# Second cross attention of a fused decoder block: scores from split keys and queries in three products, low parts on VectorE, and the last layer norm's steps in other places

## The chip, the cores and the metric

One core of a Trainium2 chip runs the whole program, one launch. The metric is the device time in microseconds (us). The times quoted are medians over runs of the same kernel. The engines are TensorE (PE, with its weight loads PEld), VectorE (DVE), ScalarE (ACT), GpSimd (POOL) and SyncE (SP, which issues DMAs here).

## What is computed

`x` is 8 batches of 256 rows of 256 features. Four residual blocks follow each other: a cross attention, a self attention with a mixture of experts, a second cross attention, and a feed-forward. The change is about the third, with its tail end in the layer norm ahead of the fourth and its preparation in the experts' stage:

```
q = rms_norm(x @ wq)                 # 16 heads of 128, rotary afterwards
k = rms_norm(x @ wk); v = x @ wv     # 4 key/value heads, 4 query heads share one
k_ctx = rms_norm(ctx @ wk_ctx)       # 64 context keys, no rotary
scores = q . concat(k_ctx, k) / sqrt(128) + causal mask on the last 256
out = softmax(scores) @ concat(v_ctx, v);  x = x + tanh(g) * (out @ wo)
x = x + tanh(g2) * ffn(layernorm(x))
```

Scores are wanted at close to full fp32 precision.

## The kernel before, in words

Stage "x1" is the second cross attention. It has 32 steps (`NI`), one for each pair of a key/value head `g = i // 8` and a batch `i % 8`; a step does the four query heads `h` of that pair. The order on every engine is written out by hand: each engine's function has a loop over `i`, and in it work for step `i` (softmax, values, output projection), `j = i + 1` (transposes of queries and keys, first scores) and `k = i + 2` (projections, rotary) is mixed. Engines meet by semaphores in the dictionary `q`; a wait blocks everything behind it on the same engine.

Products that must be precise are done with split operands: `three` adds high x high, high x low and low x high, where the high part is the operand rounded to float32r (lines L293 to L295). Where an operand isn't split, a plain fp32 matmul is issued. Before the change the scores (`scores`, L1798 and L1800) are two plain fp32 products for a head: 128 queries against 192 keys and 128 queries against 320 keys (64 context keys with 128 or 256 own ones). Stationary is the query block, moving are the keys.

The way of a query to its scores: `proj_q` on PE, `take_q` on DVE, `sum_q` on POOL, `q_tr` (four transposes for each half `t`) on PE into one of the two PSUM banks `pT`, `q_ev` (L1689) on ACT copies it to SBUF as `x_qT`. Keys go the same way by `rotate_k`, `sum_k`, `k_tr`, `k_ev` (L1696, `x_kT`); context keys are put into `x_kT` by POOL (`context_keys`, L1725). The softmax of a head is `scores` (PE), `soft` (DVE L1997), `exp` (ACT L1913), `recip` (DVE L2005), `normalise` (ACT L1921), `p_tr` (PE L1808), `p_ev` (ACT L1907), `p_low` (DVE L2010). Then `attend` (PE), `o_ev` (ACT), `o_low` (DVE L2016), `out_proj` (PE), `add_out` (DVE L2023). All transposes share the two `pT` banks in the order of the table `turns`; `bank_free` makes a transpose wait until the bank's former content has been read.

Steps 26 to 31 also carry the layer norm of the next stage, for one batch each: statistics (`norm.stats`, DVE), inverse (`norm.inverse`, POOL L190 and L192), rows (`norm_rows`, DVE L197), transposes (`norm_tr`, PE), a copy and a rounding (`norm_ev`, ACT L1941 and L1944), the low part (`norm_low`, POOL L2103).

The stage ahead, "moe", ends with the projections and transposes of step 0. At its start SP issues the loads of the experts' second bias (`moe_b`), the context and its key and value weights, tables, and of `moe_xs` (L2204).

Of the kernel before, what the change touches and what calls it, by code (L numbers as in the profile page):

```python
# [31 lines left out]
G = 4  # L32
# [38 lines left out]
def build(nc, d, out, spill, stop=99):  # L71
    ctx = ExitStack()
    with ctx:
# [1496 lines left out]
        Head = namedtuple("Head", "q QR qT kT Vh Vl KR nrq at_p at_qk bank_free place proj_kv proj_q q_tr k_tr take_kv squares q_ev k_ev "  # L1570
                          "take_q rotate_k context_keys inverse_norm_k sum_k sum_q inverse_norms_q t2")

        def cross_head(scope, KT, tables):
# [12 lines left out]
            qT = sb("x1_qT", [P, HG, S], F32, scope)  # L1586
            kT = sb("x1_kT", [P, 2, 2 * SC + S], F32, scope)
# [4 lines left out]
                     "vz", "vs", "vsf", "vsh", "pl")  # L1592
# [92 lines left out]
            def q_ev(e, i, t):  # L1685
# [3 lines left out]
                e.activation(qT[:, :, t * P:(t + 1) * P], pT[:, c % 2, :].rearrange("p (h n) -> p h n", h=HG),  # L1689
                             ACT.Copy).then_inc(q["te"], 1)  # L1690

            def k_ev(e, i):
# [3 lines left out]
                e.activation(kT[:, i % 2, SC:SC + S], pT[:, c % 2, 0:S], ACT.Copy).then_inc(q["te"], 1)  # L1696
# [57 lines left out]
            return Head(q, QR, qT, kT, Vh, Vl, KR, nrq, at_p, at_qk, bank_free, place, proj_kv, proj_q, q_tr, k_tr, take_kv, squares, q_ev,  # L1754
                        k_ev, take_q, rotate_k, context_keys, inverse_norm_k, sum_k, sum_q, inverse_norms_q, t2)

        def cross_attention_1(scope, head, KT, VC, mask, w_here, cw_here, w_next, cw_next):
# [3 lines left out]
            (q, QR, qT, kT, Vh, Vl, KR, nrq, at_p, at_qk, bank_free, place, proj_kv, proj_q, q_tr, k_tr, take_kv, squares, q_ev, k_ev, take_q,  # L1761
# [4 lines left out]
            WO = KD * (GW + 2 * HD)  # L1766
            VS = sb(name + "_VS", [P, T, HD], F32, scope)
# [11 lines left out]
            xa = KT[:, 2, :].rearrange("p (k n) -> p k n", k=KD)  # L1779
# [14 lines left out]
            def pe(e):  # L1794
                def scores(i, h):
                    e.wait_ge(q["te"], at_qk(i, 2) + 1)
                    e.wait_ge(q["sct"], pos(HG * i + h - 1))
                    e.matmul(pS[:, h % 2, 0:SC + P], qT[:, h, 0:P], kT[:, i % 2, SC + P:2 * SC + S],  # L1798
                             start=True, stop=True)
                    e.matmul(pS[:, h % 2, SC + P:2 * SC + P + S], qT[:, h, P:S], kT[:, i % 2, 0:SC + S],  # L1800
                             start=True, stop=True).then_inc(q["sc"], 1)
# [10 lines left out]
                def attend(i, hp):  # L1812

                    m = PR * i + hp
                    e.wait_ge(q["pl"], HG * i + 2 * hp + 2)
# [45 lines left out]
                for i in range(NI):  # L1861
# [28 lines left out]
                    if i >= 26:  # L1890
                        norm_tr(i - 26)
                    p_tr(i, 3)
                    if one:
                        scores(j, 1)
                    if two:
                        proj_q(e, k, 1)
# [5 lines left out]
            def act(e):  # L1902
# [34 lines left out]
                def norm_ev(b):  # L1937
                    c = place["norm", b]
                    e.wait_ge(q["tr"], c + 1)
                    e.wait_ge(q["nlo"], b)  # L1940
                    e.activation(xa, pT[:, c % 2, :].rearrange("p (k n) -> p k n", k=KD), ACT.Copy  # L1941
                                 ).then_inc(q["te"], 1)
                    e.wait_ge(q["te"], c + 1)
                    e.activation(XTh[:, :, columns(b)], xa, ACT.Copy).then_inc(q["nhi"], 1)  # L1944
# [5 lines left out]
                for i in range(NI):  # L1950
# [23 lines left out]
                    if i >= 26:  # L1974
                        norm_ev(i - 26)
# [5 lines left out]
                    if one:  # L1981
                        exp(j, 1)
                    o_ev(i, 1)
# [4 lines left out]
            def dve(e):  # L1988
# [18 lines left out]
                def p_low(i, h):  # L2007
# [3 lines left out]
                                    ).then_inc(q["pl"], 1)  # L2011
# [14 lines left out]
                def norm_rows(b):  # L2026
# [829 lines left out]
```

## Time and profile before

| | us |
|---|---|
| median of three runs (1768.93 to 1772.77) | 1770.06 |
| the profiled execution, as timed | 1772.32 |
| its span in the trace | 1770.5 |

| engine | busy us | share |
|---|---|---|
| PE | 1667.2 | 94% |
| PEld | 1514.9 | 86% |
| ACT | 1309.1 | 74% |
| DVE | 1181.1 | 67% |
| POOL | 1128.4 | 64% |

The shares are means over stages of different kinds. Stage x1 runs from 1083.19 us of the span to about 1652 us. For a stage made of equal steps the thing to read is one step: which engine has no idle time in it, and which waits of the others lead back to it. Matmuls are pipelined, so a PE record is longer than the time to the next start; what a matmul costs in a stream is start to start.

### The profile page before, as it was taken

What the parts mean: (1) busy time and instruction counts of PE and PEld (TensorE: products, weight loads), DVE (VectorE), ACT (ScalarE), POOL (GpSimd) and SP (SyncE); (2) the same over time, 40 slices, a digit from 0 to 9 for tenths busy, and PEclk for the clock granted to TensorE, in tenths of its full rate; (3) what the DMA queues carried; (4) which work ended last, traced back from release to release, by engine and by line L of the source; (5) the groups of instructions that cost most, each with busy time, mean ns of one, the idle gap of its engine ahead of it and who ended that gap; (6) DMA issues with size and microseconds to landing.
All of it is one profiled execution on the core that took longest, in us unless ns stands there. A gap on an engine that the chain in (4) does not pass through costs nothing.

```text
span 1770.5 us, 35509 instructions
## 1 busy us (share of the span) xinstructions
PE 1667.2 (94%) x11136; PEld 1514.9 (86%) x11136; DVE 1181.1 (67%) x3199; ACT 1309.1 (74%) x4211; POOL 1128.4 (64%) x1287
## 2 busy tenths in 40 slices
PE   6899998799999999999997997999999999988898
PEld 3788887688999999999986885999999999977897
DVE  5567678577776666566776786777777777776322
ACT  5677777598888888878874555889889898888221
POOL 5445546899999989898952215565565565665455
PEclk8999999899999999999998998999999999999999
DMA  4111211100000000000002010000000000000000
GB/s 147 50 42 34 70 28 59 38 19 13 19 19 13 24 15 19 14 19 13 13 7 95 20 30 8 13 13 9 13 9 12 13 9 19 19 17 8 10 19 25
DMA packets 32842, 45.88 MB, mean 26 GB/s; under 512 B 5264, under 2 KB 21904, under 8 KB 32656
## 3 DMA queue, kind: packets, MB, share of 16 engines
q1 hardware_dynamic: 32656, 43.59, 8.2%
q8 instruction: 93, 1.52, 0.4%
q14 instruction: 93, 0.76, 0.1%
HBM read 39.39 MB, written 4.19 MB: 25 GB/s over the span
## 4 chain that ended last, share of the span: by engine, by line
PE 73%; POOL 8%; DVE 8%; ACT 6%; issue 4%; DMA 1%; SPq 0%; POOLq 0%; DVEq 0%; ACTq 0%
PE pA L293 5%; PE pA L294 5%; PE pA L295 5%; PE pS L1112 4%; PE pF L293 4%; PE pF L295 4%; PE pF L294 4%; PE pS L1800 3%; PE pA L626 3%; PE pA L627 3%; PE pA L628 3%; PE pO L1131 3%; PE pF L827 3%; PE pT L1808 3%; PE pO L293 2%
## 5 line engine op out<-in xcount | busy, mean ns | idle before, releaser
L293 PE MATMUL pA<-Wh,XTh 128*128 128x512 f32 (+1 forms) x512 | 221.1, 432 | 7.8 <-SPq L119 4.2
L1533 POOL TENSOR_TENSOR f_sw<-f_sw,f_sin 128x512 f32<-128x512 f32 x128 | 181.9, 1421 | 34.1 <-ACT f_sw L1242 34.1
L294 PE MATMUL pA<-Wl,XTh 128*128 128x512 f32 (+1 forms) x512 | 188.9, 369 | 0.0
L295 PE MATMUL pA<-Wh,XTl 128*128 128x512 f32 (+1 forms) x512 | 188.6, 368 | 0.0
L1242 ACT ACTIVATE f_sw<-pA 64x512 f32<-64x512 f32 x256 | 151.8, 593 | 34.8 <-PE pA L628 31.0
L1536 POOL TENSOR_TENSOR f_sw<-f_sw,f_RB 128x512 f32<-128x512 f32 x128 | 169.5, 1325 | 10.0
L626 PE MATMUL pA<-XTh,Wh 128*128 128x256 f32 x512 | 163.8, 320 | 5.3 <-DVE f_qT L1385 5.3
L1913 ACT ACTIVATE x_P<-x_P,x_nm 128x192 f32<-128x192 f32 (+1 forms) x256 | 127.9, 505 | 51.7 <-DVE x_nm L1997 51.7
L1741 POOL TENSOR_TENSOR x_QR<-x_QR,x_t 128x512 f32<-128x512 f32 x64 | 82.1, 1283 | 118.6 <-DVE x_QR L1706 118.6
L628 PE MATMUL pA<-XTh,Wl 128*128 128x256 f32 x512 | 145.9, 285 | 0.0
L627 PE MATMUL pA<-XTl,Wh 128*128 128x256 f32 x512 | 145.8, 285 | 0.0
L1263 ACT ACTIVATE f_P<-f_P,f_nm 128x128 f32<-128x128 f32 (+1 forms) x256 | 114.0, 447 | 21.4 <-DVE f_nm L1402 21.3
L1921 ACT ACTIVATE x_P<-x_P,x_rs 128x192 f32<-128x192 f32 (+1 forms) x256 | 117.2, 515 | 10.5 <-DVE x_rs L2005 10.5
L293 PEld LDWEIGHTS pA<-Wh,XTh 128*128 128x128 f32 x512 | 98.0, 192 | 28.1 <-SPq L119 4.4
L1997 DVE CUSTOM_DVE_ANT_0 x_P<-pS,x_mask,x_nrq 128x192 f32<-128x192 f32 (+1 forms) x256 | 113.1, 478 | 7.1 <-PE pS L1800 4.2
L294 PEld LDWEIGHTS pA<-Wl,XTh 128*128 128x128 f32 x512 | 98.2, 192 | 19.0 <-issue 0.4
L2010 DVE TENSOR_TENSOR Wl<-pT,Wh 128x512 fp32r<-128x512 f32 x128 | 87.1, 680 | 38.1 <-ACT Wh L1907 37.9
L295 PEld LDWEIGHTS pA<-Wh,XTl 128*128 128x128 f32 x512 | 97.9, 191 | 17.1
L1402 DVE CUSTOM_DVE_ANT_0 f_P<-pS,f_mask 128x128 f32<-128x128 f32 (+1 forms) x256 | 80.7, 352 | 46.7 <-PE pS L1112 45.9
L1112 PE MATMUL pS<-f_kT,f_qT 128*128 128x128 f32 (+1 forms) x512 | 105.2, 328 | 3.9 <-POOL f_kT L1539 3.9
L626 PEld LDWEIGHTS pA<-XTh,Wh 128*128 128x128 f32 x512 | 98.7, 193 | 8.2 <-issue 5.7
L288 POOL TENSOR_TENSOR Wl<-RAW,Wh 128x384 fp32r<-128x384 f32 (+3 forms) x72 | 75.4, 1047 | 44.2 <-ACT Wh L281 27.4
(318 smaller groups left out, 6308.0 us busy)
## 6 DMA issues: line engine op xcount, KB each, us to landing
RAW<-in_w_f SPq DMA_DIRECT2D x32, 256.0 KB, 2.7
RAW<-in_w_x SPq DMA_DIRECT2D x32, 192.0 KB, 2.4
RAW<-in_w_x SPq DMA_DIRECT2D x32, 160.0 KB, 2.4
x_base<-in_w_x0b SPq DMA_DIRECT2D x20, 192.0 KB, 2.5
RAW<-in_w_ff SPq DMA_DIRECT2D x8, 288.0 KB, 2.8
R<-in_x SPq DMA_DIRECT2D x4, 512.0 KB, 6.8
x_spill<-R SPq DMA_DIRECT2D x8, 256.0 KB, 2.0
RAW<-in_w_moe SPq DMA_DIRECT2D x8, 256.0 KB, 2.7
```

The source lines that it names most:

```text
L293: e.matmul(o, ah, bh, start=first, stop=False)
L294: e.matmul(o, ah, bl, start=False, stop=False)
L295: return e.matmul(o, al, bh, start=False, stop=last)
L626: e.matmul(o[:, a * S:(a + 1) * S], Wh[g % 2][:, w], xh, start=(k == 0), stop=False)
L627: e.matmul(o[:, a * S:(a + 1) * S], Wh[g % 2][:, w], xl, start=False, stop=False)
L628: ins = e.matmul(o[:, a * S:(a + 1) * S], Wl[g % 2][:, w], xh, start=False, stop=(k == KD - 1))
L1112: ins = e.matmul(pS[:, h % 2, OFF[t]:OFF[t] + WID[t]], qT[:, i % 2, h, t * P:(t + 1) * P], kT[:, i % 2, h, 0:WID[t]], start=True, stop=True)
L1242: ins = e.activation(sw[dst, n, :, :], pA[src, n % 2, :].rearrange("p (a n) -> p a n", a=2), ACT.Copy)
L1533: e.tensor_tensor(y, y, bc(sind[:, :], 1, 2), ALU.mult).then_inc(q["swm"], 1)
L1536: e.tensor_tensor(y, y, RB[:, g % 2, 2 * n:2 * n + 2, :], ALU.add).then_inc(q["swb"], 1)
L1913: ins = e.activation(x, x, ACT.Exp, scale=-1.0, bias=nm[:, h, t:t + 1], accum_out=sm[:, h, t:t + 1])
L1921: ins = e.activation(x, x, ACT.Copy, scale=rs[:, h, t:t + 1])
```

## The change

Scores are computed by `three` from split operands. The ACT copies `q_ev` and `k_ev` now write the high parts `x_qTh` and `x_kTh` in float32r, and three new DVE instructions in a step write the low parts from PSUM: `q_low` twice (128x512) and `k_low` once (128x256). `scores` waits for them by the new semaphore `low`, which takes the place of `pl` and counts the low parts of all transposes in order of `turns`; `bank_free` waits for it too. POOL writes two instructions for the context keys in place of one. In the loop of DVE both `q_low` stand ahead of `rotate_k`, and `k_low` behind `p_low(i, 2)`. In the last six steps the norm's rows go from DVE to POOL, its low part from POOL to DVE (straight from PSUM, without the copy on ACT), and its transposes stand later in `turns`, on PE and on ACT. To make room in SBUF, the experts' second bias is loaded in four pieces, some of the experts' small tiles share memory, and the value weights of the context are loaded later, into the tile of the key weights.

```diff
@@ cross_head
-                turns += [("q", x, 2) for x in j] + [("norm", i - 26)] * (i >= 26) + [("p", i, 3)]
+                turns += [("q", x, 2) for x in j] + [("p", i, 3)] + [("norm", i - 26)] * (i >= 26)
+            def low_done(c):
+
+                return sum(x[0] != "norm" for x in turns[:c + 1])
             def bank_free(e, c):
 
                 e.wait_ge(q["te"], pos(c - 1))
-                if c >= 2 and turns[c - 2][0] == "p":
-                    e.wait_ge(q["pl"], HG * turns[c - 2][1] + turns[c - 2][2] + 1)
+                e.wait_ge(q["low"], low_done(c - 2) if c >= 2 else 0)
+                if c >= 2 and turns[c - 2][0] == "norm":
+                    e.wait_ge(q["nlo"], turns[c - 2][1] + 1)
...
+            def q_low(e, i, t):
+                c, x = at_qk(i, t), slice(t * P, (t + 1) * P)
+                e.wait_ge(q["te"], c + 1)
+                e.tensor_tensor(lows["q"][:, :, x], pT[:, c % 2, :].rearrange("p (h n) -> p h n", h=HG),
+                                qTh[:, :, x].bitcast(F32), ALU.subtract).then_inc(q["low"], 1)
+
+            def k_low(e, i):
+                c = at_qk(i, 2)
+                e.wait_ge(q["te"], c + 1)
+                e.tensor_tensor(kTl[:, i % 2, SC:SC + S], pT[:, c % 2, 0:S], kTh[:, i % 2, SC:SC + S].bitcast(F32),
+                                ALU.subtract).then_inc(q["low"], 1)
...
-                e.tensor_copy(kT[:, i % 2, :].rearrange("p (a n) -> p a n", n=SC)[:, ::5, :],
-                              bc(KT[:, g, b * SC:(b + 1) * SC], 1, 2))
+                e.tensor_copy(hi, own).then_inc(q["ckh"], 1)
+                e.wait_ge(q["ckh"], i + 1)
+                e.tensor_tensor(lo, own, hi.bitcast(F32), ALU.subtract)
@@ cross_attention_1, pe
                 def scores(i, h):
-                    e.wait_ge(q["te"], at_qk(i, 2) + 1)
+                    e.wait_ge(q["low"], low_done(at_qk(i, 2)))
                     e.wait_ge(q["sct"], pos(HG * i + h - 1))
-                    e.matmul(pS[:, h % 2, 0:SC + P], qT[:, h, 0:P], kT[:, i % 2, SC + P:2 * SC + S],
-                             start=True, stop=True)
-                    e.matmul(pS[:, h % 2, SC + P:2 * SC + P + S], qT[:, h, P:S], kT[:, i % 2, 0:SC + S],
-                             start=True, stop=True).then_inc(q["sc"], 1)
+                    for t, own in enumerate((slice(SC + P, 2 * SC + S), slice(0, SC + S))):
+                        r = slice(t * P, (t + 1) * P)
+                        ins = three(e, pS[:, h % 2, OFF[t]:OFF[t] + WID[t]], qTh[:, h, r], qTl[:, h, r],
+                                    kTh[:, i % 2, own], kTl[:, i % 2, own], True, True)
+                    ins.then_inc(q["sc"], 1)
@@ cross_attention_1, dve
                     soft(i, 3)
+                    if one:
+                        q_low(e, j, 0)
+                        q_low(e, j, 1)
                     if two:
                         rotate_k(e, k)
                     recip(i, 3)
-                    if i >= 26:
-                        norm_rows(i - 26)
                     o_low(i, 0)
                     p_low(i, 2)
+                    if one:
+                        k_low(e, j)
...
                     o_low(i, 1)
+                    if i >= 26:
+                        norm_low(i - 26)
@@ cross_attention_1, pool
                         sum_k(e, k)
+                    if i >= 26:
+                        norm.inverse(e, i - 26)
+                        norm_rows(i - 26)
                     w_low(i)
...
-                    if i >= 26:
-                        norm_low(i - 26)
-                    if 25 <= i < NI - 1:
-                        norm.inverse(e, i - 25)
@@ experts, sp
-                e.dma_start(b2[:, :], d["be2"].partition_broadcast(P)).then_inc(q["bias"], 16)
+                for x in range(E):
+                    e.dma_start(biases[x], d["be2"][x * D:(x + 1) * D].partition_broadcast(P)).then_inc(q["bias"], 16)
...
-                e.dma_start(wv, d["x1_Wv"].rearrange("(k p) n -> p k n", p=P)).then_inc(q["ctx"], 16)
...
+                    if i == 2:
+                        e.wait_ge(q["ck"], 4)
+                        e.dma_start(wv[:, :, :], d["x1_Wv"].rearrange("(k p) n -> p k n", p=P)).then_inc(q["wv"], 16)
@@ experts, dve, at its end
                 norm_rows(B - 1)
+                head.q_low(e, 0, 0)
+                head.q_low(e, 0, 1)
                 head.rotate_k(e, 1)
                 norm_low(B - 1)
+                head.k_low(e, 0)
```

What stands in a row on VectorE in the middle of an ordinary step, from the end of the fourth head's `soft` to `add_out`, before (L1715 to L1719 are `rotate_k`, L2005 is `recip`, L2016 `o_low`, L2010 `p_low`, L2023 `add_out`):

```order
L1997 ISA x_nm 128x1
L1715 SCALAR_TENSOR_TENSOR x_KR<-pA,x_ssk,x_cosk 128x128
L1717 SCALAR_TENSOR_TENSOR x_tk<-pA,x_ssk,x_sink 128x128
L1715 SCALAR_TENSOR_TENSOR x_KR<-pA,x_ssk,x_cosk 128x128
L1717 SCALAR_TENSOR_TENSOR x_tk<-pA,x_ssk,x_sink 128x128
L1719 TENSOR_TENSOR x_Vl<-pA,x_Vh 128x256
L2005 RECIPROCAL x_rs<-x_sm 128x2
L2016 TENSOR_TENSOR x_OTl<-pO,x_OTh 128x512
L2010 TENSOR_TENSOR Wl<-pT,Wh 128x512
L2023 SCALAR_TENSOR_TENSOR R<-pF,tanhg,R 128x512
```

The same place on VectorE in the changed kernel (its line numbers are some 15 to 25 higher; L1708 is `q_low`, L1714 is `k_low`):

```order
L2017 ISA x_nm 128x1
L1708 TENSOR_TENSOR x_qTl<-pT,x_qTh 128x4x128 x2
L1734 SCALAR_TENSOR_TENSOR x_KR<-pA,x_ssk,x_cosk 128x128
L1736 SCALAR_TENSOR_TENSOR x_tk<-pA,x_ssk,x_sink 128x128
L1734 SCALAR_TENSOR_TENSOR x_KR<-pA,x_ssk,x_cosk 128x128
L1736 SCALAR_TENSOR_TENSOR x_tk<-pA,x_ssk,x_sink 128x128
L1738 TENSOR_TENSOR x_Vl<-pA,x_Vh 128x256
L2025 RECIPROCAL x_rs<-x_sm 128x2
L2036 TENSOR_TENSOR x_OTl<-pO,x_OTh 128x512
L2030 TENSOR_TENSOR Wl<-pT,Wh 128x512
L1714 TENSOR_TENSOR x_kTl<-pT,x_kTh 128x256
L2043 SCALAR_TENSOR_TENSOR R<-pF,tanhg,R 128x512
```

Two 128x512 instructions came in ahead of the keys' rotation, and one of 128x256 behind the third head's low part; nothing else moved there.

On TensorE, at the first head's scores of the next step, between `out_proj` (pF) and `proj_q` (pA), before:

```order
L295 MATMUL pF<-Wh,x_OTl 128x256
L1798 MATMUL pS<-x_kT,x_qT 128x192
L1800 MATMUL pS<-x_kT,x_qT 128x320
L293 MATMUL pA<-Wh,XTh 128x512
L294 MATMUL pA<-Wl,XTh 128x512
```

The same place on TensorE in the changed kernel:

```order
L295 MATMUL pF<-Wh,x_OTl 128x256
L293 MATMUL pS<-x_kTh,x_qTh 128x192
L294 MATMUL pS<-x_kTl,x_qTh 128x192
L295 MATMUL pS<-x_kTh,x_qTl 128x192
L293 MATMUL pS<-x_kTh,x_qTh 128x320
L294 MATMUL pS<-x_kTl,x_qTh 128x320
L295 MATMUL pS<-x_kTh,x_qTl 128x320
L293 MATMUL pA<-Wh,XTh 128x512
```

Six products stand where two stood, and they now need the DVE rows L1708 and L1714 of the fence above; the neighbours are the same.

On GpSimd in one of the last six steps, from the queries' sums on, before (L2103 is `norm_low`, L190 and L192 `norm.inverse`, L1730 and L1732 the inverse norms of the keys for which `rotate_k` waits):

```order
L1741 TENSOR_TENSOR x_QR<-x_QR,x_t 128x512 x2
L1747 TENSOR_SCALAR x_nrq<-x_ssq 128x8
L1750 TENSOR_TENSOR x_nrq<-x_nrq,mhalf 128x8
L1752 TENSOR_SCALAR x_nrq<-x_nrq 128x8
L2103 TENSOR_TENSOR XTl<-x_KT,XTh 128x2x256
L190 TENSOR_SCALAR rstd<-mv 128x2
L192 TENSOR_TENSOR rstd<-rstd,mhalf 128x2
L1730 TENSOR_SCALAR x_ssk<-x_ssk 128x2
L1732 TENSOR_TENSOR x_ssk<-x_ssk,mhalf 128x2
```

And in the changed kernel, from the queries' inverse norms to the norm's work of the next step:

```order
L1774 TENSOR_SCALAR x_nrq<-x_nrq 128x8
L1752 TENSOR_SCALAR x_ssk<-x_ssk 128x2
L1754 TENSOR_TENSOR x_ssk<-x_ssk,mhalf 128x2
L2112 TENSOR_SCALAR x_VS<-x_VC,x_half 128x128 x2
L2116 CAST Wh<-x_VS 128x256
L2118 TENSOR_TENSOR Wl<-x_VS,Wh 128x256
L1746 CAST x_kTh<-x_KT 128x2x64
L1748 TENSOR_TENSOR x_kTl<-x_KT,x_kTh 128x2x64
L1758 TENSOR_TENSOR x_KR<-x_KR,x_tk 128x256
L190 TENSOR_SCALAR rstd<-mv 128x2
L192 TENSOR_TENSOR rstd<-rstd,mhalf 128x2
L197 TENSOR_SCALAR x_KT<-R,mv,rstd 128x256 x2
```

The low part and the inverse are gone from the place ahead of the keys' inverse norms; the inverse now stands with the rows behind the keys' sum.

## Rows read from the trace of the kernel before

**Rows 1.** Busy time (count) by engine in one step: start:end, length, PE to POOL, clock, DMA, GB/s.

```profile
1308.36:1325.26 16.90, 16.90 (x116) 15.38 (x115) 12.48 (x37) 15.10 (x56) 9.80 (x15) 1.00 0.04 11
```

**Rows 2.** Chain that ended last, 1300 to 1340 us: start, us, what.

```profile
1308.53 0.33 PE pS L1798 x2
1308.85 0.54 PE pS L1800 x2
...
1325.42 0.33 PE pS L1798 x2
```

**Rows 3.** Waits, 1110 to 1540 us: us in total, times, longest us.

```profile
ACT x_P L1913 <- DVE x_nm L1997: 32.8, 25, 1.3
```

**Rows 4.** Timeline of PE in a step: start us, us, engine, line, operation.

```profile
1308.36 0.49 PE L1798 MATMUL pS<-x_kT,x_qT 128*128 128x192 f32 x2
...
1309.46 0.39 PE L294 MATMUL pA<-Wl,XTh 128*128 128x512 f32 x1
...
1310.39 0.39 PE L295 MATMUL pA<-Wh,XTl 128*128 128x512 f32 x1
...
1317.08 0.28 PE L293 MATMUL pA<-Wh,XTh 128*128 128x256 f32 x1
...
1317.67 0.28 PE L295 MATMUL pA<-Wh,XTl 128*128 128x256 f32 x1
1317.80 0.60 PE L1808 MATMUL pT<-ident,x_P 128*128 128x128 f32 x4
```

**Rows 5.** Timeline of ACT, same step and the one before.

```profile
1301.52 0.60 ACT L1907 ACTIVATE Wh<-pT 128x512 fp32r<-128x512 f32 x1 [0.17 <-PE pT L1808]
...
1304.56 1.09 ACT L1689 ACTIVATE x_qT<-pT 128x512 f32<-128x512 f32 x2
...
1307.45 0.42 ACT L1696 ACTIVATE x_kT<-pT 128x256 f32<-128x256 f32 x1
...
1310.36 0.46 ACT L1913 ACTIVATE x_P<-x_P,x_nm 128x192 f32<-128x192 f32 x1 [1.34 <-DVE x_nm L1997]
...
1318.43 0.60 ACT L1907 ACTIVATE Wh<-pT 128x512 fp32r<-128x512 f32 x1 [0.16 <-PE pT L1808]
```

**Rows 6.** Timeline of DVE in the same step.

```profile
1305.00 0.35 DVE L1715 SCALAR_TENSOR_TENSOR x_KR<-pA,x_ssk,x_cosk 128x128 f32<-128x128 f32 x1 [0.86 <-POOL x_ssk L1732]
...
1306.05 0.42 DVE L1719 TENSOR_TENSOR x_Vl<-pA,x_Vh 128x256 fp32r<-128x256 f32 x1
...
1307.14 0.69 DVE L2016 TENSOR_TENSOR x_OTl<-pO,x_OTh 128x512 fp32r<-128x512 f32 x1 [0.32 <-ACT x_OTh L1928]
1307.75 0.68 DVE L2010 TENSOR_TENSOR Wl<-pT,Wh 128x512 fp32r<-128x512 f32 x1
...
1312.02 0.15 DVE L2005 RECIPROCAL x_rs<-x_sm 128x2 f32<-128x2 f32 x1
1312.10 0.67 DVE L2010 TENSOR_TENSOR Wl<-pT,Wh 128x512 fp32r<-128x512 f32 x1
1312.68 0.41 DVE L1997 CUSTOM_DVE_ANT_0 x_P<-pS,x_mask,x_nrq 128x192 f32<-128x192 f32 x1
```

**Rows 7.** Timeline where PE waited for ACT, first step of the stage.

```profile
1090.03 0.90 ACT L1921 ACTIVATE x_P<-x_P,x_rs 128x192 f32<-128x192 f32 x2
...
1090.98 0.33 PE L1808 MATMUL pT<-ident,x_P 128*128 128x128 f32 x1 [1.17 <-ACT x_P L1921]
```

**Rows 8.** Chain that ended last, 1540 to 1600 us, in the last six steps.

```profile
1556.85 1.68 POOL x_nrq L1750
1558.86 1.25 POOL XTl L2103
...
1576.60 1.68 POOL x_nrq L1750
```

**Rows 9.** Timelines of SP's issues and of DVE at the start of stage moe.

```profile
944.84 0.45 SPq L2204 DMA_DIRECT2D moe_xs<-x_spill  x1
...
951.93 1.79 DVE L2411 SCALAR_TENSOR_TENSOR moe_xs<-moe_b,moe_gcomb,moe_xs 128x256 f32<-128x256 f32 x2 [3.19 <-DMA moe_xs<-x_spill]
```

More of the change, by code:

```diff
@@ L1568, in feed_up @@
             ins.then_inc(ff_up["gu"], 1)
-        Head = namedtuple("Head", "q QR qT kT Vh Vl KR nrq at_p at_qk bank_free place proj_kv proj_q q_tr k_tr take_kv squares q_ev k_ev "
+        Head = namedtuple("Head", "q QR qTh kTh kTl lows low_done q_low k_low Vh Vl KR nrq at_p at_qk bank_free place proj_kv proj_q q_tr k_tr take_kv squares q_ev k_ev "
                           "take_q rotate_k context_keys inverse_norm_k sum_k sum_q inverse_norms_q t2")
@@ L1752, in inverse_norms_q @@
                 e.tensor_scalar(a, a, -1.0, None, ALU.mult).then_inc(q["rq"], 1)
-            return Head(q, QR, qT, kT, Vh, Vl, KR, nrq, at_p, at_qk, bank_free, place, proj_kv, proj_q, q_tr, k_tr, take_kv, squares, q_ev,
+            return Head(q, QR, qTh, kTh, kTl, lows, low_done, q_low, k_low, Vh, Vl, KR, nrq, at_p, at_qk, bank_free, place, proj_kv, proj_q, q_tr, k_tr, take_kv, squares, q_ev,
                         k_ev, take_q, rotate_k, context_keys, inverse_norm_k, sum_k, sum_q, inverse_norms_q, t2)
@@ L1760, in cross_attention_1 @@
             name = "x1"
-            (q, QR, qT, kT, Vh, Vl, KR, nrq, at_p, at_qk, bank_free, place, proj_kv, proj_q, q_tr, k_tr, take_kv, squares, q_ev, k_ev, take_q,
+            (q, QR, qTh, kTh, kTl, lows, low_done, q_low, k_low, Vh, Vl, KR, nrq, at_p, at_qk, bank_free, place, proj_kv, proj_q, q_tr, k_tr, take_kv, squares, q_ev, k_ev, take_q,
              rotate_k, context_keys, inverse_norm_k, sum_k, sum_q, inverse_norms_q, t2) = head
@@ L2024, in add_out, with norm_low @@
                                            ALU.mult, ALU.add).then_inc(q["acc"], 1)
-                def norm_rows(b):
-                    if b >= 2:
-                        e.wait_ge(q["tr"], place["norm", b - 2] + 1)
-                    else:
-                        e.wait_ge(q["rope"], NT * 8 * (G - 1))
-                    norm.rows(e, b)
+                def norm_low(b):
+                    c = place["norm", b]
+                    e.wait_ge(q["te"], c + 1)
+                    e.tensor_tensor(XTl[:, :, columns(b)], pT[:, c % 2, :].rearrange("p (k n) -> p k n", k=KD),
+                                    XTh[:, :, columns(b)].bitcast(F32), ALU.subtract).then_inc(q["nlo"], 1)
                 soft(0, 0)
@@ L2099, in w_low, with norm_rows @@
                     low_w(e, q["hi"], q["split"], cw_next if g == G - 1 else cw_here, i, i % 2, g % 2)
-                def norm_low(b):
-                    e.wait_ge(q["nhi"], b + 1)
-                    e.tensor_tensor(XTl[:, :, columns(b)], xa, XTh[:, :, columns(b)].bitcast(F32),
-                                    ALU.subtract).then_inc(q["nlo"], 1)
+                def norm_rows(b):
+                    if b >= 2:
+                        e.wait_ge(q["tr"], place["norm", b - 2] + 1)
+                    else:
+                        e.wait_ge(q["rope"], NT * 8 * (G - 1))
+                    norm.rows(e, b)
                 sum_q(e, 1, 0)
@@ L2402, in bias @@
                     if c == 0:
-                        e.wait_ge(q["bias"], 16)
+                        e.wait_ge(q["bias"], 64)
                         e.wait_ge(q["comb"], 1)
```

55 lines of the change are left out of this document (29 added, 26 removed).

## The prediction, made before the changed kernel ran

> **What bounds the kernel now.** I read the busy time by engine over one step first. In a step of the second cross attention PE has no idle time at all: 16.90 us of 16.90, at full granted clock, with ACT at 15.10, DVE at 12.48 and POOL at 9.80 [rows 1]. The reader is to see two things there: PE sets the step, and ACT has only 1.8 us of slack. The chain that ended last agrees: it repeats every 16.89 us, and the scores stand in it [rows 2]. Then the waits: the longest regular one of ACT is for `soft` of the next step's first head, 1.3 us at most, 25 times [rows 3]. So ACT's chain hangs on the moment at which PE gives those scores. The timelines of PE, ACT and DVE in one step then give the start of each instruction, which is all that the sum below needs [rows 4 to 6]. There are 32 steps: the first two, 25 equal ones (2 to 26), and the rest, which carry the norm in full.
>
> **The change, part by part.**
>
> *Scores, cost on PE.* Before, a head's scores take 0.33 + 0.54 = 0.87 us [rows 2]. After, they are three products of 192 columns and three of 320. What a split product costs start to start is seen at two sizes: 256 columns take 0.118 us (1317.08 to 1317.67 in five starts) and 512 take 0.2325 us (1309.46 to 1310.39 in four) [rows 4]. A line through both gives 0.147 us at 320 and 0.090 at 192. Nothing under 256 columns is in this trace in float32r, so 192 is unknown: at the low end 0.090 from the line, at the high end of what I call undisturbed 0.118 (it costs what 256 does), and, far off, the rate of plain fp32, 0.33 us for 192 columns [rows 2]. I take 0.109, near the upper of the close ends, because a weight load goes with each product. Then a head costs 3 x (0.109 + 0.147) = 0.77 us, 0.10 less than before; four heads make 0.40 us a step.
>
> The Trainium skill, page "TensorE: Matmul & The Clock Gate", section "LDWEIGHTS (loading the stationary operand)", gives columns / 1.2 ns for a load, which is 107 ns for the 128 columns here, more than the line's 90 ns. By the line the step below would come out 0.16 us shorter than by the load. The rows at 256 and 512 columns cannot tell the two apart.
>
> *Low parts, cost on DVE.* Two `q_low` have the shape of `p_low`, which takes 0.58 us start to start (1312.10 to 1312.68), and `k_low` has that of L1719, 0.42 us to its end [rows 6]. DVE has the room in total: 12.48 + 1.6 of 16.9. The cost is where they stand. They are on the way to the scores, and DVE is in order.
>
> *The new wait.* Take the step before as it ran. `k_ev` ended at 1307.45 + 0.42 = 1307.87 [rows 5], and PE began the scores at 1308.36, after its own work, without a wait [rows 4]. In the changed kernel the scores wait for `k_low`, which stands behind both `q_low`, all of `rotate_k`, `recip`, `o_low` and `p_low`. The first `q_low` waits for `q_ev`. So a cycle closes over one step, and I add it up, from first scores to first scores:
>
> 1. PE from the scores to the end of `p_tr` of the second head: 1308.36 to 1317.80 + 0.60 = 1318.40, that is 10.04 us [rows 4]. Three heads' scores lie in it, each 0.10 shorter: 9.74.
> 2. Hand-over to ACT 0.03 (`p_ev` starts at 1318.43). ACT from that `p_ev` to the start of the first `q_ev`: 1301.52 to 1304.56 = 3.04, and 0.61 for the copy itself (the row merges two, 1.09), then 0.03 to DVE: 3.71 in all [rows 5]. ACT is busy all through it.
> 3. DVE: two `q_low` 1.16; `rotate_k` 1305.00 to 1306.05 and the start to start of L1719, 0.34 (0.42 less the 0.08 overlap that DVE rows show): 1.39; `recip` 0.08 (1312.02 to 1312.10); `o_low` 0.61 (1307.14 to 1307.75); `p_low` 0.58; `k_low` 0.42. Together 4.24 [rows 6].
> 4. Hand-over to PE 0.05, from the place where PE waited for ACT (1090.03 + 0.90 to 1090.98) [rows 7].
>
> The sum is 9.74 + 3.71 + 4.24 + 0.05 = 17.74 us. The small waits on the way (the keys' transposes now need the second `q_low`) add some hundredths: I take 17.8. PE's own work would be 16.5, so PE stands idle 1.3 us in each step ahead of the first scores. Behind that wait on PE stand the projections of step k, `p_tr` of the fourth head and the second scores; ACT, which already waits 1.3 us for the first head [rows 3], waits some 2 us. The step grows by 0.9, and 25 of them by 22.5 us. The bounds: 0.090 for 192 columns gives 17.65 (nine products on the path), 0.118 gives 17.9. That is 25 x 0.75 to 25 x 1.0, or 19 to 25 us. The first two steps have the wait once or so: +0.5.
>
> *The last steps.* The chain there runs over POOL and repeats in 1576.60 - 1556.85 = 19.75 us, with the norm's low part (1.25) in it [rows 8]. That low part and the inverse leave POOL's path ahead of the keys' inverse norms, and ACT loses a copy. In exchange the new cycle of 17.8 us holds here too, with the norm's low part and statistics, 0.6 and 1.0 us, on DVE ahead of the next `p_low`. Between 17.8 and 19.4; I take 19.3, a gain of about 0.4 in some three or four steps, since the stage's tail has other limits: -1.2 us. Bounds: -7 and 0.
>
> *Loads and other small parts.* The first `moe_xs` is issued at 944.84, and DVE waits 3.19 us for it [rows 9]. Four bias loads in place of one add three issues of 0.45 us ahead, the removed value weights take one away: issued 0.9 later, with 0.5 MB less in front. I take 0, bounds -1 and +1. The value weights now come between the weight stream's third and fourth issue on SP; what they could hold back is needed a batch later. At the end of that stage two `q_low` fit into DVE's wait for the keys' inverse norms, and `k_low` adds 0.4 us: +0.2. POOL's extra instruction for the context keys, under 0.5 us, lies in its 7 us of idle time; with that cover gone it would cost 0.5 a step.
>
> **The sum.** 22.5 + 0.5 - 1.2 + 0.2 = 22; as the rounding of 17.74 to 17.8 may give 1.5 us too much, I forecast +21. The profiled execution took 1772.32 around a span of 1770.5, and so would become 1793.3; the median of the runs is 1770.06, 2.3 below it, and becomes 1791. With the bounds of the parts: 1783 to 1798.
>
> **Rivals.**
>
> *The scores' narrow products run at plain fp32's rate.* Then a product of 192 columns costs 0.33 us, a head 3 x (0.33 + 0.147) = 1.43, 0.56 more than before. Three heads on the path make the cycle 17.74 + 3 x 0.66 = 19.7, +2.85 a step, 71 us over 25; with the first and last steps some 82 us: 1852. For it: every product of `three` in the trace has 256 or 512 columns, so nothing excludes it. Against: nothing in the two sizes that are there hints at a step, since half the columns take half the time. A milder form, 0.16 us (two cycles for a column, one plain fp32 record), gives 17.74 + 0.48 = 18.2: +34 us with the ends, 1804.
>
> *The wait for the low parts is hidden, and PE stays the bound.* Then each step loses 0.40 us and 32 steps 13 us: 1757, faster. It needs the cycle to be under 16.5 us, 1.3 less than I count. It decides from the point at which DVE gives `k_low` before PE has done `out_proj`, 1308.36 in the step shown; by the sum DVE gives it 1.3 us later. For it: PE is the full engine and DVE has 4 us idle. Against: that idle time lies in other places, and DVE's starts are fixed by ACT's copies. The Trainium skill, page "FP8 and Floating Point Precision", section "TensorE Precision Notes", has true fp32 as four passes; with three products in place of four passes it speaks for a gain of a quarter of the scores' time. The trace agrees with four (192 columns in 0.33 us are 4.1 cycles a column), but the quarter is spent on PE, which would wait.
>
> *The cycle is as long, but half of the growth is hidden*, as `rotate_k` no longer waits for POOL and other waits close up: within 0.2% of 1770.
>
> **Chances.** The cycle as summed 0.74; the milder form of narrow products 0.06; plain fp32's rate 0.13; hidden wait, faster, 0.04; within 0.2% 0.03. A measurement of this kernel can tell about 0.2% (3.5 us) from no change. All but the last two are slower: 0.93. The range 1783 to 1808 takes in the likeliest case with its own range (1783 to 1798) and the milder form, 0.8 together; the far form is left out.
>
> **What the changed profile would show.** Right: steps of 17.8 us at equal distance; PE idle some 1.3 us once a step, ended by DVE's low part of the keys; DVE's `rotate_k` starting without a wait for POOL; scores of a head in 0.77 us; DVE at 14 of 17.8. The narrow products are read directly, start to start. Wrong: PE full in the steps (the wait is hidden), or an idle time that another instruction ends, or last steps that grow. What would make the sum wrong is above all an ACT that catches up while PE waits, since part 2 of the cycle is 3 us of its work, and a 192-column product outside 0.09 to 0.12.

## The result, and the profile after

The changed kernel takes 1789.68 us (median of 4 runs, 1786.65 to 1790.73), the kernel before 1770.24 (4 runs): the ratio is 1.0105, 95% interval 1.0088 to 1.0123. The forecast was 1791.0. The profiled execution of the changed kernel took 1788.75 us around a span of 1786.9. Of the kernels below, one profiled execution, that of norm_only, was disturbed (granted clock 0.65) and is not read.

One step between two of its equal neighbours, busy time by engine (start:end, length, PE to POOL, clock, DMA, GB/s), the counterpart of [rows 1]:

```profile
1317.26:1335.13 17.87, 16.82 (x123) 15.80 (x123) 13.72 (x40) 15.16 (x55) 10.24 (x16) 1.00 0.03 10
```

A step has grown from 16.90 to 17.87 us at the same clock, and PE is no longer full. The waits in the equal steps, 1120 to 1540 us (us in total, times, longest), say on what it stands:

```profile
ACT x_P L1936 <- DVE x_nm L2017: 54.5, 24, 2.3
...
PEld pS L293 <- DVE x_kTl L1714: 30.1, 24, 1.3
PE pS L293 <- DVE x_kTl L1714: 25.1, 24, 1.1
```

Once a step PE waits for the keys' low part. ACT's wait for the first head's softmax has grown from 1.3 [rows 3] to 2.3. The chain that ended last (start, us, what) shows one turn of the cycle:

```profile
1299.39 0.36 PE pS L293
...
1308.82 0.45 PE pT L1831 x4
1309.32 0.46 issue
1309.78 1.08 ACT x_P L1936 x4
...
1311.65 0.79 ACT x_P L1944 x2
1312.44 0.50 ACT x_qTh L1696
1312.96 0.52 DVE x_qTl L1708
...
1314.17 0.34 DVE x_KR L1734
...
1316.31 0.47 issue
1316.79 0.43 DVE x_kTl L1714
1317.26 0.36 PE pS L293
```

Read from the top: scores, PE's work to the second head's transposition, ACT's in-order work to the copy of the queries, then on VectorE the two `q_low`, the rotation, `o_low` and `p_low` (in the issue pieces), `k_low`, and the scores again, 17.87 us later. Without the wait the pieces from 1312.96 on could run beside PE; high_only, below, shows how far they do.

### The profile page after: what moved, and what is told of

Its sections match the earlier page's. It is cut to its first block, busy times and chain, and to the rows that moved or that the text cites. A ratio compares the mean times of both kernels' runs of the same rounds, so it can differ in the third digit from the quotient of the medians.

```text
span 1786.9 us, 36146 instructions
## 1 busy us (share of the span) xinstructions
PE 1660.5 (93%) x11392; PEld 1526.4 (85%) x11392; DVE 1220.4 (68%) x3289; ACT 1306.2 (73%) x4205; POOL 1149.5 (64%) x1325
## 4 chain that ended last, share of the span: by engine, by line
PE 64%; DVE 12%; ACT 10%; POOL 7%; issue 7%; DMA 0%; SPq 0%; POOLq 0%; DVEq 0%; ACTq 0%
PE pA L293 5%; PE pA L294 5%; PE pA L295 5%; PE pS L1112 4%; PE pA L626 3%; PE pA L628 3%; PE pA L627 3%; PE pO L1131 3%; PE pF L827 3%; PE pS L293 3%; PE pF L293 2%; PE pF L295 2%; PE pF L294 2%; ACT x_P L1936 2%; PE pT L1831 2%
## 5 line engine op out<-in xcount | busy, mean ns | idle before, releaser
L293 PE MATMUL pA<-Wh,XTh 128*128 128x512 f32 (+1 forms) x512 | 198.5, 388 | 8.1 <-SPq L119 4.2
L294 PE MATMUL pA<-Wl,XTh 128*128 128x512 f32 (+1 forms) x512 | 188.3, 368 | 0.0
L295 PE MATMUL pA<-Wh,XTl 128*128 128x512 f32 (+1 forms) x512 | 187.9, 367 | 0.0
L293 PE MATMUL pS<-x_kTh,x_qTh 128*128 128x192 f32 (+1 forms) x256 | 86.8, 339 | 35.6 <-DVE x_kTl L1714 32.1
L293 PEld LDWEIGHTS pA<-Wh,XTh 128*128 128x128 f32 x512 | 97.7, 191 | 21.1 <-SPq L119 4.4
L295 PEld LDWEIGHTS pA<-Wh,XTl 128*128 128x128 f32 x512 | 97.3, 190 | 17.0
L294 PEld LDWEIGHTS pA<-Wl,XTh 128*128 128x128 f32 x512 | 97.8, 191 | 11.3
```

The lines of the kernel that those rows point to most:

```text
L293: e.matmul(o, ah, bh, start=first, stop=False)
L294: e.matmul(o, ah, bl, start=False, stop=False)
L295: return e.matmul(o, al, bh, start=False, stop=last)
```

## Experiments

The twelve runs follow in the order in which they were made; "step" is the distance of one keys' transposition from the next in the 25 equal steps. The time of before beside them was 1771.2 us (the first four), 1771.9 (the next four) and 1770.9 (the last four); ratios are to it.

**high_only.** The scores' products read only high parts (the low parts' share of the scores is left out) and wait only for ScalarE's copies:

```diff
-                    e.wait_ge(q["low"], low_done(at_qk(i, 2)))
+                    e.wait_ge(q["te"], at_qk(i, 2) + 1)
-   three(e, ..., qTh[:, h, r], qTl[:, h, r], kTh[...], kTl[...], True, True)
+   three(e, ..., qTh[:, h, r], qTh[:, h, r], kTh[...], kTh[...], True, True)
```

> The changed kernel, but all three products of the scores read the high parts (the low parts' share of the scores is left out) and the scores wait only for the copies on ScalarE, no longer for the subtractions on VectorE; six matmuls a head and all subtractions stay. Theory (a step is the chain copy, subtraction, scores: TensorE's wait for the keys' low part, 1.3 us a step, is the cost): the wait goes, and a step falls from 17.87 to between TensorE's own busy time, 17.87 - 1.3 = 16.6, and the 16.90 of before; with some 30 steps the time is 1789.7 - 30 x 1.0 = 1760, between 1751 and 1765. Rival A (the three products themselves cost TensorE more than the two plain ones, because each needs a weight load of its own): the step stays near 17.9 and the time near 1790. Rival B (VectorE's three added subtractions, 1.6 us a step, delay its softmax work whether or not the scores wait for them): the step stays above 17.4, the time above 1775.

Measured: 1763.5 us, ratio 0.996 (0.9945 to 0.9976), step 16.92. The wait accounts for 0.95 of the 0.97 us; rival A falls. But PE is still not the bound. Its chain in a step still runs over VectorE:

```profile
1307.99 0.27 DVE x_kTl L1714
1308.32 0.74 DVE R L2043
1309.06 0.32 DVE x_P L2017
...
1310.26 0.73 ACT x_P L1936 x3
...
1311.51 0.70 DVE Wl L2030
1312.26 0.50 PE pO L293
```

The subtraction that nobody waits for still stands ahead of the sum into the rows and of the softmax of the next head. Rival B is right in kind, but small.

**f32_wait.** The products are plain fp32 again, of the high parts (the low parts' share is left out); the wait stays:

```diff
-   three(e, ..., qTh[:, h, r], qTl[:, h, r], kTh[...], kTl[...], True, True)
+   e.matmul(..., qTh[:, h, r].bitcast(F32), kTh[...].bitcast(F32), start=True, stop=True)
```

> The changed kernel, but the scores are two plain fp32 matmuls of the high parts again (the low parts' share is left out), while they still wait for both subtractions. Theory (the wait is the cost, and the three products are slightly cheaper than the plain ones): a head's scores go from 0.78 back to the 0.87 of before, the wait of 1.3 us stays, and a step takes 17.9 to 18.2, the time 1790 to 1800. Rival A (the products are the cost): the step is back at 16.9 and the time at 1770.

Measured: 1797.95 us, ratio 1.0154 (1.0138 to 1.0170), step 18.14. The wait alone costs 18.14 - 16.90 = 1.24 a step; the three products give back 0.27 of it, 0.09 for each of the three heads on the cycle.

**no_q_low.** Both `q_low` are left out, and the third product reads the high queries in their place (the diff shows the loop of VectorE alone):

```diff
-                    if one:
-                        q_low(e, j, 0)
-                        q_low(e, j, 1)
```

> The changed kernel without the two subtractions of the queries' low parts (the product of low queries with high keys reads the high queries in their place, so this share of the scores is left out); the keys' subtraction and its wait stay. Theory (all that stands on VectorE between ScalarE's copies and the keys' subtraction is on the cycle): two subtractions of 0.585 us start to start leave the cycle, 17.87 - 1.17 = 16.70, near TensorE's busy 16.6, and the time is 1789.7 - 30 x 1.17 = 1755, between 1748 and 1762. Rival (the keys' subtraction waits for its own copy on ScalarE, and the queries' lie in VectorE's idle time): the step stays above 17.6, the time above 1782.

Measured: 1772.9 us, ratio 1.001 (1.0001 to 1.002), step 17.20: 0.67 of the 1.17. The step falls only as far as the next way to the scores allows. Its chain reaches `k_low` over ScalarE's next exponential and copy:

```profile
1309.53 0.62 ACT x_qTh L1696
1310.14 0.75 ACT x_P L1935 x3
1311.11 0.50 ACT x_OTh L1950
1311.63 0.69 DVE x_OTl L2035
1312.43 0.41 issue
1312.84 0.43 DVE x_kTl L1714
1313.31 0.36 PE pS L293
```

**narrow.** Each product of 320 columns becomes one of 192 and one of 128:

```diff
-   for t, own in enumerate((slice(SC + P, 2 * SC + S), slice(0, SC + S))):
+   for t, a, n, at in ((0, SC + P, SC + P, OFF[0]), (1, 0, SC + P, OFF[1]), (1, SC + P, P, OFF[1] + SC + P)):
```

> The changed kernel with each product of 320 key columns split into one of 192 and one of 128: nine matmuls a head for six, the same columns in all, three more weight loads. In the trace of the changed kernel 192 columns take 0.110 us from start to start and 320 take 0.148. Theory W (below some width the weight load of about 0.107 us sets the distance, not the columns): 128 columns take 0.107 too, a head goes from 0.78 to 9 x 0.11 = 0.98, the four heads add 0.8 us of TensorE time a step; as 1.3 us of it was idle and one head's products lie on the cycle, a step takes 18.1 to 18.8, the time 1797 to 1817. Theory C (columns alone count, 0.110 x 128/192 = 0.073): a head goes to 0.88, at most 0.1 us more on the cycle, the time 1790 to 1794.

Measured: 1809.7 us, ratio 1.0222 (1.0204 to 1.0240), step 18.57. PE's timeline of one head (start, us, line, shape):

```profile
1310.04 0.27 PE L295 MATMUL pS<-x_kTh,x_qTl 128*128 128x192 f32 x1
1310.15 0.25 PE L293 MATMUL pS<-x_kTh,x_qTh 128*128 128x128 f32 x1
1310.23 0.27 PE L294 MATMUL pS<-x_kTl,x_qTh 128*128 128x128 f32 x1
1310.34 0.28 PE L295 MATMUL pS<-x_kTh,x_qTl 128*128 128x128 f32 x1
```

Over 200 us of this trace a product of 128 columns takes a median 0.112 us from start to start where L294 or L295 issues it (0.083 for L293's), one of 192 0.111: a third fewer columns bring nothing in two of three. A head has three more products and the step 0.70 us more, as theory W had it (theory C forecast at most 0.1). Theory W holds in kind. That the weight load is what holds them was not separated from another fixed cost.

**norm_only.** The kernel before with the norm's move alone:

```diff
-                    if i >= 26:
-                        norm_tr(i - 26)
                     p_tr(i, 3)
                     if one:
                         scores(j, 1)
+                    if i >= 26:
+                        norm_tr(i - 26)
...
-                    e.activation(xa, pT[...], ACT.Copy).then_inc(q["te"], 1)
-                    e.wait_ge(q["te"], c + 1)
-                    e.activation(XTh[:, :, columns(b)], xa, ACT.Copy).then_inc(q["nhi"], 1)
+                    e.activation(XTh[:, :, columns(b)], pT[...], ACT.Copy).then_inc(q["te"], 1)
```

(with `norm_rows` and `norm.inverse` on GpSimd and `norm_low` on VectorE, as in the change).

> The kernel before with only the norm's operations of its last six steps moved as in the change (its rows on GpSimd, one copy in place of two, its low part on VectorE out of the bank, its transposition behind the last head's scores); the scores stay plain. In the changed kernel the six steps and the tail took 4.6 us less than before beyond what the longer cycle does, where 1.2 was forecast. Theory (the move shortens the chain over GpSimd by itself): the time is 1770.2 - 4.6 = 1765.6, between 1763 and 1768. Rival (the gain came only because the changed kernel's steps are longer and hide the norm): 1769 to 1772, no difference.

Measured: 1762.1 us, ratio 0.9940 (0.9926 to 0.9955): 9.8 us faster, twice what was expected. Its steps are read in norm_only_b, below.

**rotate_last.** The keys' rotation behind the keys' subtraction:

```diff
-                    if two:
-                        rotate_k(e, k)
                     recip(i, 3)
                     o_low(i, 0)
                     p_low(i, 2)
                     if one:
                         k_low(e, j)
+                    if two:
+                        rotate_k(e, k)
```

> The changed kernel with the keys' rotation on VectorE (1.41 us, five instructions) behind the keys' subtraction, where it stood ahead of it; nothing is left out. Theory (what stands on VectorE between the queries' and the keys' subtraction is on the cycle, but the rotation is itself waited for by GpSimd's sum and then by the keys' transposition, which comes next): a step falls by a part of 1.41, to between 17.4 and 17.7, the time 1778 to 1787. Rival A (the whole 1.41 leaves the cycle, and TensorE's own 16.6 is the bound): 1752. Rival B (the rotation stood in idle time of VectorE): 1790, unchanged.

Measured: 1793.2 us, ratio 1.0125 (1.0110 to 1.0140): no gain on the changed kernel, whose interval ends at 1.0123. The step is 17.61, as the theory had it, 0.26 less than in the changed kernel and far from the 1.41 that was moved. What it left out are the last steps, at 20.87, 20.86, 20.85 and 21.99 us (19.04, 19.02, 19.03 and 18.56 in the changed kernel, so 8.9 more in all): the norm's rows on GpSimd wait behind the sum that needs the rotation.

```profile
1583.22 0.34 DVE x_Vl L1738
1583.63 0.74 POOL x_KR L1758
...
1584.73 0.73 POOL rstd L192
1585.64 2.44 POOL x_KT L197 x2
1588.22 0.63 PE pT L205 x4
```

**low_first.** Only work that nobody awaits at once is moved behind the subtraction:

```diff
-                    recip(i, 3)
-                    o_low(i, 0)
                     p_low(i, 2)
                     if one:
                         k_low(e, j)
+                    recip(i, 3)
+                    o_low(i, 0)
```

> The changed kernel with the last head's low part and the keys' subtraction moved on VectorE ahead of the reciprocal and the output's low part (0.08 + 0.60 us); the rotation stays ahead; nothing is left out. Theory (the same as of the rotation, with nothing that the moved operations are awaited for at once): a step falls by 0.68 to 17.2, the time 1789.7 - 30 x 0.68 = 1769, between 1766 and 1774, level with the kernel before. Rival (the keys' subtraction waits for its copy on ScalarE, which comes no earlier): 1785 to 1790.

Measured: 1772.7 us, ratio 1.0007 (0.9998 to 1.0017), step 17.21. Two moved instructions give back 17 of the 19 us.

**best_order.** ScalarE and VectorE in another order (one step, first and last calls left out):

```diff
                     squares(e, j, 1)
-                    p_ev(i, 1)
-                    exp(i, 2)
                     take_kv(e, k)
+                    p_ev(i, 1)
+                    exp(i, 2)
-                    normalise(i, 2)
                     q_ev(e, j, 0)
                     q_ev(e, j, 1)
-                    exp(i, 3)
+                    normalise(i, 2)
                     o_ev(i, 0)
                     p_ev(i, 2)
                     k_ev(e, j)
+                    exp(i, 3)
...
                     rotate_k(e, k)
-                    recip(i, 3)
-                    o_low(i, 0)
                     p_low(i, 2)
                     k_low(e, j)
-                    add_out(i - 1)
+                    recip(i, 3)
+                    o_low(i, 0)
```

> The changed kernel with another order of work on ScalarE and VectorE, nothing left out: ScalarE takes the projected keys before the second head's copy and copies the queries before the third head's normalisation, and the fourth head's exponential comes behind the copies of the keys; on VectorE the keys' subtraction comes before the reciprocal, the output's low part and the sum into the rows. Theory (the cycle of copy, subtraction, scores is what the three products cost, and shortening what stands in it gives it back down to TensorE's busy time and the 16.9 of before): a step takes 16.9, with the norm's 4 to 5 us the time is 1770.2 - 4.6 = 1765, or less, down to 1758, since the scores are cheaper at both ends too. Rival (another chain, that of ScalarE's 15.2 us busy with softmax and copies, closes at once behind it): 1770 to 1785.

Measured: 1764.5 us, ratio 0.9954 (0.9940 to 0.9968), step 16.95. `k_low` is still once a step on the chain. The kernel is faster than the one before, but not by its products: its step is no shorter than the 16.90 of before, and norm_only, with plain fp32 products, took 1762.1 beside it. What it gains on the kernel before is no more than the norm's move gives by itself.

**norm_only_b.** The same kernel as norm_only.

> The kernel before with only the norm's move, a second time, for the steps in its trace. The first time it took 1762.1, 9.8 less than before, where 4.6 was expected. Theory (before, the last steps were paced by GpSimd's chain of the norm at up to 19.7 us; without it they fall to TensorE's 16.9, while in the changed kernel they can fall only to that kernel's own 17.9 or more): the four steps that took 18.48, 19.72, 19.74 and 19.20 before take 17 to 18 each, the time is 1762 again. Rival (the gain lies behind the last step, or in another stage): these steps stay above 18.5.

Measured: 1759.6 us, ratio 0.9943 (0.9929 to 0.9956), so again 11 us faster. The four last steps take 17.73, 18.28, 18.27 and 18.00 us, 72.3 in all for 77.1 before. Some 4.6 us more are behind the last step: from its keys' transposition to the end it is 145.5 us for 150.1. One part of them is two waits of PE for the last low parts, 2.73 and 2.12 us before (the second shown, from PE's timeline) and 1.58 and 0.98 now, since a copy and a rounding of the norm stood ahead of ScalarE's last `p_ev`:

```profile
1643.16 0.54 PE L293 MATMUL pO<-Wh,x_Vh 128*128 128x512 f32 x1 [2.12 <-DVE Wl L2010]
```

```profile
1633.08 0.50 PE L293 MATMUL pO<-Wh,x_Vh 128*128 128x512 f32 x1 [0.98 <-DVE Wl L2008]
```

The other part is PE's granted clock. The windows of 11 us that begin 20 us behind the last keys' transposition, first of before and then of norm_only_b, have 0.84 and 1.00:

```profile
1640.45:1651.45 11.00, 7.05 (x42) 6.07 (x40) 2.27 (x4) 3.79 (x6) 1.67 (x2) 0.84 0.00 0
```

```profile
1632.53:1643.53 11.00, 6.97 (x51) 6.46 (x52) 3.42 (x6) 3.29 (x7) 1.74 (x4) 1.00 0.04 13
```

So have the next 11 us (1651.45 to 1662.45 before, 0.84; 1643.53 to 1654.53 now, 1.00). Counted from the last keys' transposition, PE is 2.2 us earlier behind the two waits, 3.6 behind the first window's stretch at the lower clock (512 columns at 0.43 us there) and 5.0 behind the second's (256 columns at 0.21 and not 0.12).

**products_only.** The changed kernel with the norm as before (the edit of norm_only, undone).

> The changed kernel with the norm's operations of the last six steps put back as they were before (rows on VectorE, two copies on ScalarE, low part on GpSimd, its transposition ahead of the last head's); the three products stay. Theory (its last steps were faster by less than those of the norm's move alone, since the three products' longer cycle runs through them): the time is 1789.7 + 4.6 = 1794.3, between 1792 and 1798, so the move is worth less here than the 9.8 that it brings alone. Rival (it is worth the same in both): 1789.7 + 9.8 = 1799.5.

Measured: 1803.6 us, ratio 1.0189 (1.0175 to 1.0203). Both expectations fall: the move is worth 13.9 us here (1803.6 - 1789.7; 13.3 to 14.9 by how the two runs of before are set off). The last four steps take 20.97, 22.11, 20.64 and 20.19 us. Two of them by windows:

```profile
1586.79:1608.90 22.11, 19.16 (x127) 17.48 (x127) 15.87 (x45) 16.59 (x59) 12.94 (x19) 0.92 0.05 14
1608.90:1629.54 20.64, 17.76 (x128) 16.16 (x127) 15.87 (x45) 16.49 (x59) 12.94 (x19) 1.00 0.06 15
```

and the chain through the first of them:

```profile
1581.96 1.68 POOL x_nrq L1770
1583.97 1.26 POOL XTl L2130
1585.58 0.73 POOL rstd L192
1586.68 0.71 POOL x_ssk L1752
...
1588.94 1.06 DVE x_KT L197 x2
...
1591.19 0.34 DVE x_kTl L1712
1591.58 0.53 PE pS L293
...
1593.39 0.43 PE pA L293
```

The two cycles join: GpSimd's norm work delays the keys' inverse norms, so the rotation, and `k_low` behind it with the norm's rows (1.06) between. PE waits 2.95 us, and behind the wait its 512-column products take 0.43 us and not 0.23: the granted clock stands at the lower of its two levels, 1.2 for 2.4 GHz, for a short time. The same happens behind the wait of 2.0 us a step earlier (1572 us). It doesn't happen behind the next two, of 2.82 and 2.95 us, and the second window above, at a clock of 1.00, is long all the same: the clock is a small part of these steps.

**k_first.** The order of best_order, with the keys' transposition ahead of the third head's (`turns`, and the keys' copy and subtraction on ScalarE and VectorE, follow it):

```diff
                     attend(i, 0)
-                    p_tr(i, 2)
                     if one:
                         k_tr(e, j)
+                    p_tr(i, 2)
```

> The order of work of the run before, in which the cycle was cut, and TensorE too in another order: the keys' transposition stands ahead of the third head's, so their copy and subtraction come first as well; nothing is left out. Theory (in the run before, at 16.95 a step, the chain still went through the keys' low part once a step, and TensorE's own work is some 0.3 less than before's 16.90): a step takes 16.6 to 16.75, the time is 1764.5 - 30 x 0.3 = 1756, between 1753 and 1761. Rival (16.95 is TensorE's own work with three products, its busy time was 16.82): 1761 to 1766, no difference from the run before.

Measured: 1754.0 us, ratio 0.9911 (0.9897 to 0.9924), step 16.55, with no idle time of PE left in the equal steps.

**full_order.** The PE order of one step (VectorE and ScalarE follow it):

```text
p_tr(i,0) proj_kv scores(i,2) scores(i,3) q_tr(j,0) p_tr(i,1) out_proj(0) q_tr(j,1) k_tr(j)
attend(i,0) p_tr(i,2) out_proj(1) scores(j,0) proj_q(0) p_tr(i,3) scores(j,1) proj_q(1) norm_tr attend(i,1)
```

> As the kernel with the keys' transposition first, and it now stands ahead of the first pair's attention too, the queries' transposition ahead of the second head's, the projection of keys ahead of the third head's scores, with ScalarE and VectorE ordered to match; nothing is left out. Theory (no wait is left on TensorE, its own work of 16.5 to 16.6 a step is the bound): the time is 1764.5 - 30 x 0.4 = 1752, between 1746 and 1758. Rival (TensorE's own work is 16.8): 1759 to 1763.

Measured: 1745.7 us, ratio 0.9861 (0.9847 to 0.9874), step 16.54 in most of the equal steps and 16.63 in seven: 25 us below the kernel before and 44 below the changed one. The equal steps are no shorter than in k_first; the first two take 35.6 us for k_first's 40.0 and the last four 67.6 for 72.7. Ten equal steps of it:

```profile
1244.60:1410.59 165.99, 165.99 (x1223) 157.41 (x1222) 137.04 (x391) 153.07 (x550) 102.57 (x151) 1.00 0.04 11
```

PE has no idle time again. So about 16.55 is its own work with three products, and 16.90 was that with plain fp32.

What plain fp32 products would take in this order wasn't run. PE is already full in their equal steps, so there the three products are worth 25 x 0.35 = 9 us; whether the gains of the order in the first two and last four steps need them is not shown.

## Why the prediction was right, point by point

- **Total.** 1791.0 was forecast, 1789.7 measured. The two profiled executions are 16.4 us apart (1786.9 - 1770.5): 24.2 in the 25 equal steps, -0.3 in the first two, -1.5 in the last four, -3.3 behind them, and -2.7 ahead of all, of which 2.4 arise in stages that the change doesn't touch. The forecast had 22.5, +0.5 and -1.2 in the steps and nothing behind them. So the cycle was taken 1.7 us too small over its 25 steps and what lies behind the steps was left out at 3.3; these cancel in part, and that the total came out within 1.3 us is partly luck. The range's lower end is not quite the sum of its parts: 1770 + 18.75 + 0.5 - 7 - 1 + 0.2 gives 1781.5, and 1783 was stated.
- **Scores, cost on PE.** Forecast: 0.77 us a head and 0.40 less a step. The step of k_first and full_order, where PE is full, is 0.34 us below 16.90 on the mean. In the changed kernel a head from 1320.13 to 1320.91 is 0.78:

```profile
1320.33 0.12 PE pS L295
1320.44 0.17 PE pS L293
1320.61 0.15 PE pS L294
1320.76 0.15 PE pS L295
```

  In the second and third products of three, 192 columns take 0.110 to 0.113 us start to start (0.109 taken) and 320 take 0.148 (0.147); the first of three stands apart, at 0.17 for 320 columns. Of the two readings weighed there, the 0.107 us of the Trainium skill's load (page "TensorE: Matmul & The Clock Gate", section "LDWEIGHTS (loading the stationary operand)", an estimate from its formula) is nearer than the line's 0.090; narrow's 0.112 at 128 columns agrees with such a floor, its 0.083 for the first of three does not. The rival of plain fp32's rate is excluded by the same rows.
- **The new wait.** Cycle 17.74, taken as 17.8: 17.87. Its parts: PE 9.86 us (9.74 forecast), ScalarE with the hand-overs 3.71 (3.71), VectorE 4.25 (4.24), the hand-over to PE 0.05. PE idles once a step, ended by `k_low`: 30.1 us in 24 waits by its weight loads, 1.25 each, and 25.1 or 1.05 by its products (1.3 forecast). ACT's "some 2 us": 2.3. `rotate_k` starts without a wait, as was said. high_only shows that the wait is the cost, no_q_low, low_first and rotate_last that the parts named are on the cycle, though another way closes in behind each (rotate_last got 0.26 of 1.41), and k_first that without the wait the step is 16.55. The rival of a hidden wait was right that the three products are the cheaper ones; its 0.40 us a step is some 0.34, or 9 us in the equal steps, and it needs another order of work to come true.
- **The first steps.** +0.5 was forecast. Both together took 41.54 us for 41.84. Their second is 18.4 us at a granted clock of 0.86 in both kernels, but 16.5 at 0.97 in norm_only_b, which issues there what before does, and 16.9 at 0.96 in products_only, which issues what the changed kernel does: so these two steps tell little.
- **The last steps.** 19.3 was forecast, 19.04, 19.02, 19.03 and 18.56 measured; the four gain 1.5 us (1.2 forecast). The way named is the one that ran: the new cycle, with the norm's low part (`XTl`) and statistics (`n_bst`) on VectorE ahead of `p_low` (chain that ended last: start, us, what).

```profile
1594.41 0.69 DVE x_OTl L2036
1595.10 0.60 DVE XTl L2049
1595.70 0.67 DVE n_bst L182 x2
...
1596.64 0.57 DVE Wl L2030
```

- **Behind the last step, the term put at nothing.** "the stage's tail has other limits" gave it no number, and it fell from 150.1 to 146.7 us. The causes are those of norm_only_b: shorter waits of PE for the last low parts (1.67 and 0.97 us for 2.73 and 2.12), and one stretch at the lower clock where before has two.
- **What the small net hid.** The forecast priced the last steps only net. The move brings 9.8 and 11.3 us by itself (norm_only, twice) and 13.9 beside the three products; the products without it cost 32.8 us (1803.6 - 1770.9) and not some 23: 24 of these are the cycle in the equal steps, and 6.8 are the four last steps (83.9 for 77.1), where the cycle meets GpSimd's chain. The net of these larger effects, -1.5 - 3.3, lies inside the stated bounds of -7 and 0, but the text had priced neither of them.
- **Loads and other small parts.** Forecast 0 and +0.2. From the first load of the second bias to the first keys' transposition it is 138.7 us for 139.0, and VectorE waits 2.9 us for the first `moe_xs` (3.19 before, [rows 9]). The first keys' transposition is at 1076.3 us after, 1079.0 before, and anywhere from 1075.9 to 1080.1 in the other traces, so up to 4 us of any difference of two spans says nothing on the edit.

What makes the clock fall behind one wait and not behind another of the same length stays open.

## What to carry to other kernels

A cheaper operation with a longer way to its operands is a loss where its engine is the full one: sum the cycle from the engine's use of the result to its next one, over every in-order queue between, before counting the saving. Then ask which instructions stand in that cycle only by the order in which they were written. Here reordering gave 44 us where the change had cost 19: 33 of them in the equal steps, some 14 in the first two and last four, less 3 behind those. Each reordering had to be summed for the last steps too, where rotate_last lost what it had won. Price two edits that meet on one engine together: taken alone they came to 32.8 - 10.5 = 22 us, together to 19. And compare a bundle with its best part: best_order beat the kernel before, but not the norm's move alone.

## What was not expected of the hardware

A wait can cost more than its own length, and its length doesn't say whether: in the last steps of products_only waits of 2.0 and 2.95 us were followed by a stretch in which 512 columns took 0.43 us and not 0.23, and waits of 2.82 and 2.95 us were not. Behind the stage the same wait of 2.06 us was followed by such a stretch in before, where waits of 2.12 and 1.41 us had come ahead of it, and not in norm_only_b, where 0.98 and 1.41 had. Waits of 1.1 to 1.3 us once a step left the granted clock at 1.00 (the changed kernel). Narrow split products gain nothing from width: 128 and 192 columns both take 0.11 us as the second and third of three; only the first is quicker, 0.083 at 128.
